# Twelve of the first batch's sixteen value pages loaded by SyncE, one in each of the units 82 to 93

## The chip, the core and the metric

The kernel runs on one core of a Trainium2 chip. The metric is the device time of one execution in microseconds; of the kernel before there are three runs, 997.36 to 998.01, with the median 997.86. The core has TensorE (PE, with PEld for the loads of its weights), VectorE (DVE), ScalarE (ACT), GpSimd (POOL) and SyncE (SP, which here only issues DMAs and waits), and 16 DMA engines that all queues share. Each engine runs its own list of instructions in order; they meet at semaphores.

## What is computed

A batch of 32 sequences of 32 tokens with 512 features gets a residual of a small per-subject matrix product (layer 0) and then a residual of attention over a paged cache (layer 1). Cut to what matters here:

```python
# x: (32, 32, 512); block_table: (32, 16) page numbers below 64
x = x + einsum('bct,bcd->bdt', x, weights[subjects])       # layer 0
q = rope(rmsnorm(x @ Wq.T)); k = rope(rmsnorm(x @ Wk.T)); v = x @ Wv.T
kc = k_cache[block_table].reshape(32, 512, 8, 128)         # 16 pages of 32 rows
vc = v_cache[block_table].reshape(32, 512, 8, 128)
k_all, v_all = concat(kc, k), concat(vc, v)
probs = softmax(where(valid, q @ k_all * SCALE, -1e30))    # 32 query heads on 8 key heads
x = x + (probs @ v_all) @ Wo.T
```

## The kernel before

**Stages.** The first stage runs 96 units (NU), twelve weight chunks by eight groups of four batches (NG = 8): units 0 to 79 (NN = 80) project queries and keys, units 80 to 95 the new values. A unit is twelve matmuls of 512 columns on TensorE. Beside them ScalarE and VectorE turn both caches into pairs of 16-bit numbers, high and low part, which SyncE stores into two tensors in device memory: k_pages_t (keys, one block per page) and v_pages, (2048 rows, 2048 elements), whose row is one cached token: 8 heads by high and low part by 128, 4096 bytes. A page is 32 rows, 128 KB.

The second stage is the attention: 256 steps i and a few to drain, four query heads of one batch to a step, eight steps to a batch. In step i TensorE does the transposes of the softmax rows of step i (L1585), the scores of step i + 3 (L1571 and L1575), and from step 3 on the products with the values of an earlier step (L1614); VectorE takes the maxima (L1267), ScalarE the exponentials (L1039), POOL multiplies the rows by the reciprocals of their sums (norm, L957). The scores of the steps 0 to 2 are computed already in the units 93 to 95.

**Where keys and values lie.** kt[b % 2] holds the keys of batch b, vs[b % 2] its values: `vs0` is 128 partitions by four chunks c of 4096 bytes; chunk c holds the pages 4c to 4c + 3, each on 32 partitions. TensorE's first scores of a batch wait for all its 16 key pages and its new keys (d_kt, 17 DMAs), its first product with values for the four gathers of the batch (d_vs).

**POOL.** After the last unit of the projections of keys, POOL waits for the stored caches (converted), for the row numbers v_row and for VectorE's count of 80 tiles (v_proj), then issues the four gathers of batch 0 (load_v, L944), each 128 rows by 4096 bytes by row number. Then it normalises rows 0 and 1, and in step 0 of its loop: row 2, a wait for the new values of batch 0 (d_vn, L989), a wait for the last projection (L993), the first gather of batch 1, and on to row 3.

**SyncE.** Its list is written out by hand, unit by unit. In unit u from 80 to 95 (NEXT_KEYS_AT = 80) it reads one page number into a register (TENSOR_LOAD, L716) and loads one key page of batch 1 (L721). In the units 84, 86 and 88 it loads 1 MB of output weights, four heads at a time (WO_LOADS, L734); ScalarE and VectorE convert two heads in each of the units 89 to 94 (L1082, L1315), so the third load is wanted in unit 93. In unit 83 it stores the row scales and in unit 87 loads them (L774), followed in unit 87 by the queries and new keys of batches 0 and 1 (L708, L710). In unit 93 it loads the new values of batch 0 (load_new_v, L730, three DMAs of 64 KB). Each unit ends with the store of the new values that VectorE staged for the unit before (v_new, L805, 256 KB), for which SyncE waits on v_proj. Behind the last unit: the last such store (L811), two more loads of output weights, a wait until all stores have landed, the new values of batch 1 (L730), and then for each batch b the queries of batch b + 2 (L708, after TensorE's count of scores), its 16 key pages (L721) and its new values.

## Time and profile before

| | |
|---|---|
| median of three runs | 997.86 us (997.36 to 998.01) |
| the profiled execution | 997.4 us, span of the core 995.6 us, mean granted TensorE clock 0.998 |
| TensorE matmuls, weight loads | 959.1 us busy (96%), 797.6 us (80%) |
| VectorE, ScalarE, POOL | 828.0 us (83%), 761.1 us (76%), 579.0 us (58%) |
| DMA | 294.92 MB, mean 296 GB/s over the span |
| SyncE's and ScalarE's DMA queue, POOL's queue | 76.4% and 18.2% of the 16 DMA engines' time |

All times below are microseconds from the start of the span. A line of a timeline has start, duration, engine, line of the code, operation, output <- input, and in brackets how long the engine was idle before and what ended that. SPq is SyncE's list of DMA issues; the duration of an issue is SyncE's own time, not that of the transfer. A DMA share of 1.00 means that all 16 DMA engines are busy. The projections end and the attention begins between about 338 and 356 us.

### The profile page before, as it was taken

What the parts mean: (1) busy time and instruction counts of PE and PEld (TensorE: products, weight loads), DVE (VectorE), ACT (ScalarE), POOL (GpSimd) and SP (SyncE); (2) the same over time, 40 slices, a digit from 0 to 9 for tenths busy, and PEclk for the clock granted to TensorE, in tenths of its full rate; (3) what the DMA queues carried; (4) which work ended last, traced back from release to release, by engine and by line L of the source; (5) the groups of instructions that cost most, each with busy time, mean ns of one, the idle gap of its engine ahead of it and who ended that gap; (6) DMA issues with size and microseconds to landing.
All of it is one profiled execution on the core that took longest, in us unless ns stands there. A gap on an engine that the chain in (4) does not pass through costs nothing.

```text
span 995.6 us, 25120 instructions
## 1 busy us (share of the span) xinstructions
PE 959.1 (96%) x8075; PEld 797.6 (80%) x8075; DVE 828.0 (83%) x1842; ACT 761.1 (76%) x2108; POOL 579.0 (58%) x861
## 2 busy tenths in 40 slices
PE   6899999999899999899999999999999999989998
PEld 4678888888677778788888888888888888878885
DVE  7789999999998689888878888888887887877880
ACT  5898999988884688888777778777877777777770
POOL 5565665655893057666755666565556555655550
PEclk9999999999999999999999999999999999999999
DMA  5899999989998989999999998999998999999950
GB/s 195 285 307 338 320 381 374 383 286 379 399 365 264 342 306 352 342 308 269 292 313 270 289 304 285 296 295 271 329 269 274 334 283 260 308 291 284 262 133 11
DMA packets 249907, 294.92 MB, mean 296 GB/s; under 512 B 79024, under 2 KB 206512, under 8 KB 247216
## 3 DMA queue, kind: packets, MB, share of 16 engines
q1 hardware_dynamic: 231088, 226.07, 76.4%
q0 software_dynamic: 18688, 67.25, 18.2%
q8 instruction: 65, 1.06, 0.4%
q14 instruction: 66, 0.54, 0.2%
HBM read 231.77 MB, written 46.27 MB: 279 GB/s over the span
## 4 chain that ended last, share of the span: by engine, by line
PE 75%; DVE 10%; POOL 6%; issue 5%; ACT 2%; DMA 2%; SPq 0%; DVEq 0%; ACTq 0%; POOLq 0%
PE ps_proj L1533 17%; PE ps_y L1533 16%; PE ps_o L1614 14%; PE ps_s L1571 8%; PE ps_t L1585 7%; PE ps_s L1575 7%; PE ps_rt L1709 2%; POOL vs L944 2%; DVE c_stage L1429 1%; POOL probs L963 1%; DVE rot L1405 1%; PE ps_o L1626 1%; DVE rot L1397 1%; DVE probs L1267 1%; DVE stage L1415 1%
## 5 line engine op out<-in xcount | busy, mean ns | idle before, releaser
L1039 ACT ACTIVATE probs<-probs,neg_max 128x544 f32<-128x544 f32 x256 | 191.6, 749 | 114.1 <-DVE neg_max L1267 97.3
L1267 DVE CUSTOM_DVE_ANT_0 probs<-ps_s,mask,row_scale 128x544 f32<-128x544 f32 x256 | 200.5, 783 | 52.3 <-PE ps_s L1575 41.2
L1614 PE MATMUL ps_o<-pt,vs 128*128 128x128 f16 x3072 | 213.3, 219 | 0.9 <-DMA vs<-v_pages,v_row 0.8
L1614 PEld LDWEIGHTS ps_o<-pt,vs 128*128 128x128 f16 x3072 | 192.4, 98 | 15.8 <-DMA vs<-v_pages,v_row 1.6
L963 POOL TENSOR_SCALAR probs<-probs,recip 128x512 f32<-128x512 f32 x144 | 99.8, 693 | 167.8 <-DVE recip L1275 164.2
L909 POOL TENSOR_TENSOR roped<-rot 128x256 f32<-128x256 f32 x160 | 144.1, 922 | 79.9 <-DVE rot L1397 75.9
L1533 PE MATMUL ps_proj<-wt_hi,x0t_hi 128*128 128x512 f32 x384 | 159.1, 415 | 6.2 <-DVE x0t_lo L1223 5.8
L1287 DVE SCALAR_TENSOR_TENSOR pt<-ps_t,pt 128x512 f16<-128x512 f32 x190 | 130.4, 686 | 36.7 <-ACT pt L1045 30.9
L1533 PE MATMUL ps_y<-wo,ot_hi 128*128 128x512 f16 x512 | 153.3, 381 | 0.0
L1533 PE MATMUL ps_proj<-wt_hi,x0t_lo 128*128 128x512 f32 x384 | 150.7, 394 | 0.0
L1533 PE MATMUL ps_proj<-wt_lo,x0t_hi 128*128 128x512 f32 x384 | 149.8, 391 | 0.0
L944 POOL DMA_INDIRECT vs<-v_pages,v_row x128 | 130.8, 1022 | 27.7 <-issue 9.4
L1571 PE MATMUL ps_s<-kt,qt 128*128 128x256 f16 (+1 forms) x768 | 136.0, 286 | 0.8 <-issue 0.7
L1045 ACT ACTIVATE pt<-ps_t 128x512 f16<-128x512 f32 x190 | 112.0, 590 | 24.9 <-PE ps_t L1585 18.3
L1575 PE MATMUL ps_s<-kt,qt 128*128 128x288 f16 (+1 forms) x768 | 125.8, 273 | 1.5 <-DVE neg_max L1267 1.4
L1585 PE MATMUL ps_t<-fixed,probs 128*128 128x128 f32 x760 | 115.5, 275 | 7.8 <-POOL probs L963 4.8
L1585 PEld LDWEIGHTS ps_t<-fixed,probs 128*128 128x128 f32 x760 | 91.9, 141 | 35.0 <-POOL probs L963 6.5
L1114 ACT ACTIVATE squares<-ps_proj 128x128 bf16<-128x128 f32 x320 | 85.3, 297 | 23.3 <-PE ps_proj L1533 23.2
L1533 PE MATMUL ps_y<-wo,ot_lo 128*128 128x512 f16 x256 | 97.0, 379 | 0.0
L1575 PEld LDWEIGHTS ps_s<-kt,qt 128*128 128x128 f16 x768 | 73.7, 98 | 20.2 <-DVE neg_max L1267 3.9
L1533 PEld LDWEIGHTS ps_proj<-wt_hi,x0t_hi 128*128 128x128 f32 x384 | 72.4, 189 | 20.9 <-DVE x0t_lo L1223 7.1
L957 POOL TENSOR_SCALAR probs<-probs,recip 128x544 f32<-128x544 f32 (+1 forms) x64 | 43.3, 676 | 76.1 <-DVE recip L1275 74.2
(162 smaller groups left out, 1811.8 us busy)
## 6 DMA issues: line engine op xcount, KB each, us to landing
kt<-k_pages_t SPq DMA_DIRECT2D x512, 128.0 KB
c_nat<-in_L_cond_k_cache SPq DMA_DIRECT2D x32, 512.0 KB, 6.0
q_t<-stage SPq DMA_DIRECT2D x64, 256.0 KB, 6.3
c_nat<-in_L_cond_v_cache SPq DMA_DIRECT2D x32, 512.0 KB, 7.2
qt<-q_t SPq DMA_DIRECT2D x32, 512.0 KB
w_nat<-in_L_cond_Wq SPq DMA_DIRECT2D x8, 1024.0 KB, 7.5
k_pages_t<-c_stage SPq DMA_DIRECT2D x16, 512.0 KB, 5.2
c_nat<-in_L_cond_Wo SPq DMA_DIRECT2D x16, 512.0 KB, 6.5
```

What stands on the lines that cost most here:

```text
L909: last = pool.tensor_tensor(dst, a, b, ALU.add)
L944: pool.indirect_dma_start(vs[b % 2][:, c].rearrange("p j s d -> p (j s d)"), None, v_pages, bass.IndirectOffsetOnAxis(ap=v_row[:, b * NCH ...
L963: pool.tensor_scalar(old_keys(i), old_keys(i), col(recip, i), 1.0, ALU.mult, ALU.mult).then_inc(p_old, 1)
L1039: act.activation(pr, pr, ACT.Exp, bias=col(neg_max, i), scale=-1.0, accum_out=col(row_sum, i)).then_inc(a_exp, 1)
L1045: act.activation(pt_part(i, 0), t_bank("t", i)[:], ACT.Copy, scale=P_SCALE).then_inc(a_thi, 1)
L1267: dve.tensor_tensor_reduce(out=probs_of(i), in0=ps_s[:, score_cols(i):score_cols(i) + KEYS], in1=mask[(i // HK) % 2][:, mask_at(i):mask_at ...
L1287: dve.scalar_tensor_tensor(pt_part(i, 1), t_bank("t", i)[:], P_SCALE, pt_part(i, 0), ALU.mult, ALU.subtract).then_inc(v_tlo, 1)
L1533: ins = pe.matmul(ps, a, b, start=first and n == 0, stop=last and n == len(pairs) - 1)
L1571: pe.matmul(own[0], q[:, a], k[:, b, own[1]:own[2]], start=n2 == 0, stop=n2 == 2)
L1575: ins = pe.matmul(shared[0], q[:, a], k[:, b, shared[1]:shared[2]], start=n2 == 0, stop=n2 == 2)
L1585: ins = pe.transpose(t_bank("t", i)[:, c * P:(c + 1) * P], probs_of(i)[:, SEQ * (i % 2) + c * P:SEQ * (i % 2) + (c + 1) * P], ident[:])
L1614: ins = pe.matmul(ps_o[n % 2][:, jl * P:(jl + 1) * P], v[:, part, :], pt[pt_slot(i)][:, NCH * half + c, :], start=jl == 1 and c == 0 and k ...
```

## The change

SyncE gets a second helper, load_value_pages, which reads one page number into a register and loads that page's 32 rows, 128 KB, into the 32 partitions and the chunk of vs[0] where they belong. It is called in each of the units 82 to 93, behind the key page of the unit, for the pages 4 to 15; in unit 82 SyncE first waits for VectorE's count of 80 tiles. POOL's gather for batch 0 keeps the chunk 0 alone. The first product with the values of batch 0 waits for the twelve pages (a semaphore of their own, d_vp) and for the one gather; the counts of the later even batches are three DMAs lower.

```diff
+    d_vp = sem("d_vp")
...
+    VALUES_AT = 82
...
+            def load_value_pages(first, count):
+
+                _, pages = nc.values_load_multi_w_load_instructions(
+                    page_ids[0:1, first:first + count], engines=[SP_ENGINE], min_val=0, max_val=PAGES - 1,
+                    skip_runtime_bounds_check_because="page_ids is clamped to the pages on the vector engine")
+                rows_of_page = v_pages.rearrange("(n t) f -> n t f", t=PSIZE)
+                for pg, page in enumerate(pages, first):
+                    c, a = divmod(pg, GB)
+                    sp.dma_start(vs[0][PSIZE * a:PSIZE * (a + 1), c].rearrange("p j s d -> p (j s d)"),
+                                 rows_of_page[bass.ds(page, 1)].rearrange("a t f -> (a t) f")).then_inc(d_vp, 16)
...
                 if NEXT_KEYS_AT <= u < NEXT_KEYS_AT + NPP:
                     load_pages(1, u - NEXT_KEYS_AT, 1)
+                if u == VALUES_AT:
+                    sp.wait_ge(v_proj, NN)
+                if VALUES_AT <= u < VALUES_AT + NPP - GB:
+                    load_value_pages(u - VALUES_AT + GB, 1)
...
             pool.wait_ge(v_proj, NN)
-            load_v(0, *range(NCH))
+            load_v(0, 0)
...
                 if j == 1:
-                    pe.wait_ge(d_vs[b % 2], 16 * NCH * (b // 2 + 1))
+                    if b == 0:
+                        pe.wait_ge(d_vp, 16 * (NPP - GB))
+                    pe.wait_ge(d_vs[b % 2], 16 * (NCH * (b // 2 + 1) - (0 if b % 2 else NCH - 1)))
```

## Rows read from the trace of the kernel before

**Rows 1.** Windows of core 0: length, busy us of each engine, PEclk, DMA share, GB/s.

```profile
312.00:330.00 18.00, 18.00 (x81) 14.52 (x80) 10.31 (x24) 6.14 (x10) 0.00 (x0) 1.00 1.04 353
330.00:344.00 14.00, 14.00 (x67) 11.17 (x65) 10.82 (x17) 11.54 (x19) 0.00 (x0) 1.00 1.05 385
344.00:352.00 8.00, 6.52 (x41) 4.46 (x38) 5.77 (x15) 5.64 (x12) 1.45 (x2) 1.00 0.34 105
352.00:376.00 24.00, 22.81 (x259) 20.13 (x258) 20.98 (x59) 20.26 (x48) 15.67 (x20) 1.00 1.02 347
```

**Rows 2.** Timeline of TensorE's weight loads (start, us, what, idle before, releaser).

```profile
375.36 0.22 PEld L1571 LDWEIGHTS ps_s<-kt,qt 128*128 128x128 f16 x3 [0.36 <-DMA kt<-k_pages_t]
```

**Rows 3.** Timeline of POOL, 305 to 354 us: gathers L944, normalisations L957.

```profile
305.80 1.11 POOL L944 DMA_INDIRECT vs<-v_pages,v_row  x1 [0.17 <-issue]
...
349.02 0.72 POOL L957 TENSOR_SCALAR probs<-probs,recip 128x544 f32<-128x544 f32 x1 [38.38 <-DVE recip L1275]
...
352.21 0.72 POOL L957 TENSOR_SCALAR probs<-probs,recip 128x544 f32<-128x544 f32 x1 [1.05 <-DVE recip L1275]
...
353.08 1.02 POOL L944 DMA_INDIRECT vs<-v_pages,v_row  x1 [0.15 <-issue]
```

**Rows 4.** Timeline of TensorE: the fourth transposes of the attention.

```profile
354.96 0.63 PE L1585 MATMUL ps_t<-fixed,probs 128*128 128x128 f32 x4 [0.63 <-issue]
```

**Rows 5.** Timeline of SyncE's DMA issues, 330 to 370 us.

```profile
330.35 0.34 SPq L734 DMA_DIRECT2D wo<-in_L_cond_Wo  x1
...
332.32 0.53 SPq L805 DMA_DIRECT2D v_new<-stage  x1
...
333.32 0.34 SPq L721 DMA_DIRECT2D kt<-k_pages_t  x1
...
333.72 0.53 SPq L805 DMA_DIRECT2D v_new<-stage  x1
...
340.47 1.27 SPq L730 DMA_DIRECT2D vn<-v_new  x3
...
351.09 0.51 SPq L811 DMA_DIRECT2D v_new<-stage  x1
...
354.39 1.28 SPq L730 DMA_DIRECT2D vn<-v_new  x3
...
358.34 0.34 SPq L708 DMA_DIRECT2D qt<-q_t  x1
...
360.52 9.10 SPq L721 DMA_DIRECT2D kt<-k_pages_t  x16
```

**Rows 6.** Time to landing: wo issued 330.35, wo issued 351.65 and 352.3, v_new issued 346.83.

```profile
DMA to landing us min/median/max: 8.4/8.4/8.4
...
DMA to landing us min/median/max: 6.0/6.0/6.0
...
DMA to landing us min/median/max: 2.4/2.4/2.4
```

**Rows 7.** Line L716, 305 to 345 us: SyncE's reads of page numbers, ns min/median/max.

```profile
L716 SPq TENSOR_LOAD <-page_ids x16: 265/274/907, 305.3 to 344.1; - x16
```

**Rows 8.** SyncE's waits, 305 to 330, then 330 to 360 us (total, times, longest).

```profile
SPq L751 <- DVE stage L1415: 5.1, 2, 3.4
...
SPq L811 <- DVE stage L1409: 3.7, 1, 3.7
...
SPq L708 <- PE ps_s L1575: 2.7, 1, 2.7
...
SPq L805 <- DVE stage L1409: 2.3, 2, 1.9
...
SPq L730 <- DMA v_new<-stage: 0.5, 1, 0.5
```

**Rows 9.** Timelines of VectorE and of ScalarE before the attention.

```profile
337.69 0.35 DVE L1505 TENSOR_SCALAR row_scale<-row_scale,s_unscale 128x256 f32<-128x256 f32 x1
...
341.61 1.32 ACT L1082 ACTIVATE wo<-wo,scale 128x512 f16<-128x512 f32 x2
```

## The prediction

> **What bounds the kernel now.** I read the windows table first. In the second half of the projections, 312 to 344 us, TensorE is busy every microsecond at the full clock (1.00, the 2.4 GHz level), and it is so again from 352 to 376 us apart from small gaps; between lies the turn from the projections to the attention, 344 to 352, where it loses about 1.5 us [rows 1]. The same table shows the second resource: the 16 DMA engines are full (1.04, 1.05) up to 344, nearly idle (0.34) from 344 to 352, and full again (1.02, 347 GB/s) from 352 to 376 [rows 1]. So until 344 no value load can be worth anything to TensorE, while after 352 TensorE and the DMA engines are both at their limit. Where do they meet? TensorE's weight load at 375.36, the first of batch 2's scores, waited 0.36 us and was released by the landing of batch 2's key pages [rows 2]. Those pages have no slack at all: that is the place by which I judge this change.
>
> **POOL's side.** Before, POOL issues four gathers from 305.80 on, about 1 us each, and then has nothing to do until the first softmax rows at 349.02; its work on batch 1's values begins at 353.08, right behind its third normalisation at 352.21 [rows 3]. Three gathers fewer cost POOL nothing and give nothing: the cover is its own idle time. The values of batch 0 are first read in step 3 of the attention, after TensorE's transposes at 354.96 [rows 4], and the last of the twelve pages is issued in unit 93, which is about 349 in the working below. With the 5.7 us that follow as the nearest latency (key page issues end at 360.52 + 9.10 = 369.62 and TensorE is released at 375.36 [rows 2, 5]) the last page would land at about 355, just in time; with the 2.4 us of a lightly loaded engine [rows 6], at 351.5. I take the light value, for the engines drain in this stretch. No gain, no cost.
>
> **SyncE's side.** A unit without a wait is one key page and one store of new values: from the store at 332.32 to the one at 333.72 are 1.40 us, of which the store takes 0.53, so a page costs SyncE 0.87 (0.34 for the issue at 333.32, the read of the page number, 0.274 in the middle of 16 such reads, and the steps between) [rows 5, 7]. A value page is the same pair of instructions, so I take 0.87. Bounds: 0.34 + 0.27 = 0.61 if the steps overlap, and 0.53 + 0.53 = 1.06 if its issue is as long as that of a store; single reads of page numbers took up to 0.907 [rows 5, 7]. The Trainium skill, "DMA: Bandwidth & Descriptors", section "Latency and other measured facts", gives a tensor_load a floor of about 600 ns; the row has 265 to 274 ns for most, so the row decides, but by the page each added page would cost 1.20 us, and SyncE would be 3.6 us later than I say.
>
> The twelve pages are in units 82 to 93. The one of unit 82 vanishes: before unit 83's store SyncE waits 3.4 us for VectorE [rows 8]. Eleven remain: 11 x 0.87 = 9.6 us. Queued behind them on SyncE are, in order:
> - the third load of output weights, issued at 330.35 behind six of the eleven (+5.2, so 335.6). It landed 8.4 us after its issue, with full engines [rows 5, 6]. ScalarE uses it at 341.61 [rows 9]. With 8.4 it would come 2.3 late; but SyncE now sends less per microsecond, so the backlog shrinks; with the 6.0 us of two such loads at 352 [rows 6] it is in time. I take 0, and keep 2.3 for the range.
> - the row scales and the queries of batch 0, +3.5: both are issued in unit 87, by 330. The scales are read by VectorE at 337.69 [rows 9], the queries by TensorE later still, in unit 93. Nothing.
> - the new values of batch 0 (340.47; a wait of 0.5 goes), +9.1: issued at 349.6 to 350.9. POOL waits for them ahead of the gather at 353.08 and of the normalisation that TensorE waits for at 354.96 (idle 0.63) [rows 3 to 5]. With the 2.4 us landing they are there at about 353.2: 0.2 to 1 us late. This one is on the path.
> - the last store of new values: it waited 3.7 us for VectorE, the one before about 1.9 [rows 8]. So 9.1 - 5.6 = 3.5 us late: 354.6 instead of 351.09.
> - two loads of output weights of 1 MB, right behind it, then batch 1's new values (354.39), then batch 2's queries and key pages, which waited 2.7 us for TensorE (358.34) [rows 5, 8]. The issue of batch 2's pages is thus only 3.5 - 2.7 = about 0.8 us late, plus what the longer landing of the last store adds: 1 to 2 us.
>
> **The sum goes by the DMA engines.** From 352 they are full, so batch 2's pages land when the bytes in front of them are through. What before was sent in the idle 344 to 352 is now sent later: of SyncE's list, one key page (128 KB) and two stores of 256 KB, some 0.65 MB, are issued after 352, at 347 GB/s 1.9 us [rows 1]. The 2 MB of output weights start 3.5 us later, and the stretch before them is fed with 384 KB per 1.40 us (0.27 of 0.35 MB per us) and one gather, so about 0.6 us of the engines is lost. Together 2.5 us; the pages had no slack [rows 2], so TensorE resumes at 375.4 + 2.5. The 0.2 to 1 us at step 3 lies ahead of this and is contained in it (TensorE comes later and waits less). Behind 376 TensorE is dense and everything that SyncE and POOL issue waits for TensorE's counts, so the shift stays: nothing gives it back. The profiled execution was 997.4 us (span 995.6 and 1.8 around it), the median of the runs 997.9; 997.9 + 2.5 = 1000.4.
>
> Bounds: with 0.61 per page, 6.7 - 0.5 - 5.6 = 0.6 us late at the last store, and the total is about +0.3. With 1.06, 11.7 - 6.1 = 5.6 late, about +4.6.
>
> **The rivals.**
> *Hidden.* SyncE's waits of 3.7, 2.3, 2.7 and 0.5 us are 9.2 together, nearly the 9.6 added [rows 8]. If the full engines before 344 are what stretches SyncE's issues (16 reads from 0.265 to 0.907), fewer bytes ahead shorten them by 1 to 2 us, the two stores go out before 352, and what remains is the 0.2 us at step 3: 998.1. For it: the added load is as large as the slack, not larger. Against it: the waits lie behind the loads, but the new values of batch 0 lie ahead of them and see the full 9.1.
> *Several things late.* Reads of 0.9 us, the third load of output weights 2.3 us late for ScalarE just when the softmax chain starts, new values 2 us late for POOL: 1.06 per page and more gives +4.6 to +6: about 1003. The Trainium skill, "SBUF — State Buffer", section "Door 1: The DMA port swizzle", says that a transfer's rate depends on how many of 16 ports its partitions reach, and 32 consecutive partitions reach 8. No row isolates a 32-partition transfer. As a mechanism of this kernel: twelve pages of 128 KB at 385 GB/s [rows 1] take 0.34 us each of the engines, at half the rate 0.68, so 4.1 us more in a stretch that was full; about half of it fits in the idle time the slower SyncE makes, the rest moves batch 2's pages: +4.5, 1002.4.
> *Faster.* The four gathers put 2 MB into the engines at 306 to 311, ahead of SyncE's list. If the later waits for DMAs come from backlog that never drains, sending 1.5 MB of it in pieces would let batch 2's pages land sooner. Place: the weight load at 375.36; price: its 0.36 us [rows 2], and at most some 2 us if other waits on values later share the cause: 996 to 997.5. It decides only if the engines have no idle time between; they have 5 us at 344 to 352 (0.34 busy) [rows 1], which wipes out any backlog. Little chance.
> *The change doesn't do what it says.* The pages might go out in one burst because SyncE waits at unit 82 for VectorE's count of 80 tiles; but POOL passed the same wait at 305.80 [rows 3], before SyncE gets there. No chance worth a number.
>
> **How the numbers follow.** Likeliest 0.60: +1 to +4, 1000.4. Hidden 0.25: within 1 us. Several late: 0.07, +4 and more; the port rule 0.03 beside it. Faster 0.05. The range of 8 in 10 runs from 997.9 (the low bound of the page's cost and the hidden case) to 1003.0 (the high bound). A measurement tells about 0.2%, 2.0 us, from no change. Of the likeliest case about three quarters lie above +2.0, and all of the two cases behind it: slower 0.55. Faster by over 2.0: 0.03. Same: 0.42.
>
> **What would show it.** SyncE's new page loads 0.87 us apart from their neighbours; the new values of batch 0 issued at 349 to 351; the last store near 354.6 with no wait before it; TensorE's weight load for batch 2's scores near 378 and released by the key pages, with a longer wait than 0.36; the windows 344 to 352 with a DMA share well over 0.34. The forecast is wrong if the last store is still released by VectorE at about 351, or if the pages land by 376 although SyncE is late: then bytes were not the limit.

## The result, and the profile after

| | before | after |
|---|---|---|
| median of the runs made beside each other | 998.01 us (13 runs, 996.50 to 999.44) | 1000.75 us (13 runs, 999.17 to 1004.55) |
| ratio with its 95% interval | | 1.0033 [1.0023, 1.0044] |
| profiled execution, its span, mean granted clock | 997.4, 995.6 us, 0.998 | 1004.55, 1002.8 us, 0.995 |
| the same kernel profiled again (e1_again, below) | | 1000.26, 998.5 us, 0.997 |

The changed kernel is slower: by 0.33% in the paired ratio, and by 2.7 us between the medians, where +2.5 us (0.25%) was forecast. Its first profiled execution was the slowest of its 13; the second, e1_again, lies near the median, and I read both.

The windows of the changed kernel that answer to [rows 1], with the same columns (length, busy us of PE, PEld, DVE, ACT, POOL, PEclk, DMA share, GB/s), first execution:

```profile
312.00:330.00 18.00, 18.00 (x81) 14.61 (x80) 10.10 (x23) 6.64 (x11) 0.00 (x0) 1.00 0.75 234
330.00:344.00 14.00, 13.74 (x65) 10.74 (x63) 9.11 (x14) 8.83 (x14) 0.00 (x0) 1.00 1.02 346
344.00:352.00 8.00, 3.24 (x10) 2.66 (x11) 4.02 (x7) 5.30 (x9) 0.00 (x0) 0.81 0.76 238
352.00:376.00 24.00, 22.74 (x237) 19.43 (x237) 20.46 (x57) 18.98 (x43) 14.37 (x19) 0.99 0.96 321
```

and of e1_again:

```profile
344.00:352.00 8.00, 5.64 (x33) 3.99 (x34) 5.75 (x14) 6.03 (x13) 1.45 (x2) 1.00 0.77 245
352.00:376.00 24.00, 22.78 (x258) 20.05 (x256) 20.99 (x58) 19.89 (x47) 15.09 (x20) 1.00 1.00 347
```

The values no longer fill the engines at 312 to 330 (0.75 instead of 1.04) and what SyncE sends late fills the gap at 344 to 352 (0.76, 0.77 instead of 0.34), as forecast. In the first execution TensorE works only 3.24 us of those 8, in the second 5.64, against 6.52 before.

Two waits carry the loss. The timelines of ScalarE and of TensorE's weight loads in the first execution (start, duration, what, and in brackets the idle time before with its releaser):

```profile
345.74 1.33 ACT L1099 ACTIVATE wo<-wo,scale 128x512 f16<-128x512 f32 x2 [4.57 <-DMA wo<-in_L_cond_Wo]
...
382.62 0.22 PEld L1588 LDWEIGHTS ps_s<-kt,qt 128*128 128x128 f16 x3 [3.13 <-DMA kt<-k_pages_t]
```

and in e1_again:

```profile
342.19 1.33 ACT L1099 ACTIVATE wo<-wo,scale 128x512 f16<-128x512 f32 x2 [1.77 <-DMA wo<-in_L_cond_Wo]
...
378.37 0.35 PEld L1588 LDWEIGHTS ps_s<-kt,qt 128*128 128x128 f16 x3 [2.78 <-DMA kt<-k_pages_t]
```

The first is ScalarE in unit 93, which before worked there at 341.61 without a wait [rows 9]: the third load of output weights comes late. The second answers to [rows 2]: batch 2's key pages, 0.36 us of waiting before, 3.13 and 2.78 now.

**How much is lost where.** Already at unit 80, ahead of the first changed instruction, the profiled executions lie up to 1.8 us to either side of the kernel before, so I count every time from ScalarE's work on unit 80. Its timeline in the kernel before, the work on unit 80 and an exponential of step 30:

```profile
301.81 0.69 ACT L1121 ACTIVATE stage<-ps_proj,scale 128x512 f16<-128x512 f32 x1 [2.19 <-PE ps_proj L1533]
...
409.43 0.75 ACT L1039 ACTIVATE probs<-probs,neg_max 128x544 f32<-128x544 f32 x1 [1.38 <-DVE neg_max L1267]
```

and in e1_again:

```profile
300.77 0.69 ACT L1138 ACTIVATE stage<-ps_proj,scale 128x512 f16<-128x512 f32 x1 [1.58 <-PE ps_proj L1550]
...
413.85 0.75 ACT L1056 ACTIVATE probs<-probs,neg_max 128x544 f32<-128x544 f32 x1 [1.59 <-DVE neg_max L1284]
```

That is 113.08 against 107.62 us: e1_again is 5.46 us late at step 30. The same count in every kernel gives a "shift" for the exponential of step 30, for that of step 224 and for the end of the span:

| kernel | third weight load issued | ScalarE's wait | last store issued | TensorE's wait, batch 2 | shift at 30 / 224 / end |
|---|---|---|---|---|---|
| before | 330.4 | none | 351.1 | 0.36 | 0 / 0 / 0 |
| after | 338.1 | 4.57 | 356.8 | 3.13 | 9.1 / 9.1 / 7.7 |
| e1_again | 337.2 | 1.77 | 355.0 | 2.78 | 5.5 / 5.4 / 3.9 |
| e2_third_ahead | 329.5 | none | 356.2 | 3.99 | 5.4 / 5.1 / 2.8 |
| e3_fifth_behind | 337.4 | 1.68 | 355.5 | 0.75 | 9.1 / 9.5 / 7.2 |
| e4_both | 328.9 | none | 354.9 | 1.47 | 5.6 / 5.6 / 3.3 |
| e5_gathers_spread | 332.8 | none | 351.2 | 0.28 | 0.1 / 0.6 / 0.6 |
| e6_reads_only (the kernel before once more) | 330.5 | none | 351.1 | none | 0.1 / -0.1 / 1.4 |
| e7_four_pages | 334.6 | 2.15 | 353.9 | 0.85 | 2.7 / 2.9 / 1.4 |
| e8_weights_behind_new_values | 337.6 | 4.83 | 357.8 | 1.79 | 7.7 / 7.7 / 5.5 |
| e9_weights_in_unit_95 | 330.3 | none | 351.1 | none | 1.0 / 1.0 / 1.0 |
| e10_issue_time_only | 338.5 | 2.03 | 358.2 | 3.67 | 9.3 / 9.1 / 10.0 |
| e11_three_small_gathers | 337.2 | 1.53 | 355.8 | 3.17 | 4.5 / 4.2 / 3.1 |
| e12_four_pages_third_ahead | 327.9 | none | 351.1 | 1.03 | 0.6 / 0.5 / -1.0 |

The loss at the front is 5.5 to 9.1 us, two to nearly four times the forecast. Between step 30 and step 224 next to nothing changes ("the shift stays"). Behind step 224 every kernel with fewer gathers than before, and e11, makes good some 2.3 us from one exponential to the next; in e1_again and in the first execution of the changed kernel 0.8 and 1.0 us of that are lost again a few steps on, where TensorE waits 0.65 and 0.82 us for values, so that 1.5 and 1.4 remain at the end. With e1_again's early unit 80 (-1.04) its 3.9 make the 2.9 us between the spans, 998.5 and 995.6.

**One execution is not the kernel.** e6_reads_only turned out to be the kernel before once more, and its trace ends 1.4 us later than that of before. TensorE waited 2.42 us in batch 27 in both; behind the wait its granted clock stayed at 1.00 in the one and fell in the other, which put 1.5 us on the exponentials. The window of e6 behind that wait:

```profile
891.00:895.00 4.00, 3.61 (x25) 3.18 (x26) 0.69 (x1) 1.08 (x2) 2.93 (x5) 0.57 0.93 282
```

A granted clock of 0.57 over 4 us is 1.7 us of the full clock lost. Such stretches stand at different places in different traces. The first execution of the changed kernel has two of them at the front (348 to 353 and 383 to 387 us), e1_again one (378 to 382), e3 three (346 to 350, and two together at 397 to 405), e4, e7 and e11 one each, e8 and e10 two each, e2, e5, e9 and e12 none. So a shift of one trace can hold up to 5 us of clock beside the waits, and differences of 1 to 2 us between shifts don't rank two kernels; the medians do.

All medians, each against runs of the kernel before on the same chip:

| kernel | median us (runs) | before | ratio |
|---|---|---|---|
| e1_again | 1001.47 (5) | 997.74 | 1.0037 [1.0024, 1.0050] |
| e2_third_ahead | 1001.86 (5) | 997.74 | 1.0044 [1.0031, 1.0057] |
| e3_fifth_behind | 1002.42 (6) | 997.74 | 1.0044 [1.0027, 1.0060] |
| e4_both | 1001.49 (7) | 997.74 | 1.0042 [1.0024, 1.0059] |
| e5_gathers_spread | 999.29 (12) | 997.52 | 1.0013 [0.9997, 1.0030] |
| e6_reads_only | 997.68 (12) | 997.52 | 1.0002 [0.9989, 1.0015] |
| e7_four_pages | 995.58 (12) | 997.52 | 0.9982 [0.9969, 0.9995] |
| e8_weights_behind_new_values | 1002.47 (6) | 997.52 | 1.0055 [1.0038, 1.0073] |
| e9_weights_in_unit_95 | 997.96 (12) | 998.17 | 1.0003 [0.9991, 1.0014] |
| e10_issue_time_only | 1006.62 (6) | 998.17 | 1.0094 [1.0074, 1.0114] |
| e11_three_small_gathers | 1000.38 (12) | 998.17 | 1.0026 [1.0013, 1.0039] |
| e12_four_pages_third_ahead | 996.06 (12) | 998.55 | 0.9978 [0.9965, 0.9991] |

### The profile page after: what moved, and what is told of

The parts are those of the page before. It is cut to its first block, busy times and chain, and to the rows that moved or that the text cites. A ratio compares the mean times of both kernels' runs of the same rounds, so it can differ in the third digit from the quotient of the medians.

```text
span 1002.8 us, 25165 instructions
## 1 busy us (share of the span) xinstructions
PE 961.1 (96%) x8075; PEld 800.1 (80%) x8075; DVE 828.2 (83%) x1842; ACT 761.9 (76%) x2108; POOL 576.3 (57%) x858
## 3 DMA queue, kind: packets, MB, share of 16 engines
q8 instruction: 65, 1.06, 0.4%
## 4 chain that ended last, share of the span: by engine, by line
PE 71%; DVE 10%; POOL 5%; issue 5%; DMA 4%; SPq 2%; ACT 2%; DVEq 0%; ACTq 0%; POOLq 0%
PE ps_proj L1550 17%; PE ps_y L1550 15%; PE ps_o L1633 13%; PE ps_s L1588 7%; PE ps_t L1602 7%; PE ps_s L1592 7%; PE ps_rt L1728 2%; DVE c_stage L1446 1%; POOL vs L961 1%; DVE probs L1284 1%; POOL probs L980 1%; DVE rot L1422 1%; DVE rot L1414 1%; PE ps_o L1645 1%; DVE stage L1432 1%
## 5 line engine op out<-in xcount | busy, mean ns | idle before, releaser
L961 POOL DMA_INDIRECT vs<-v_pages,v_row x125 | 128.0, 1024 | 24.6 <-issue 12.9
```

The source lines that it names most:

```text
L961: pool.indirect_dma_start(vs[b % 2][:, c].rearrange("p j s d -> p (j s d)"), None, v_pages, bass.IndirectOffsetOnAxis(ap=v_row[:, b * NCH ...
```

## The experiments

### e1_again: the changed kernel, unedited

> The changed kernel, not edited: a second profile of it. In the first one ScalarE waited 4.57 us for the third load of output weights (unit 93) and TensorE's weight load waited 3.13 us for batch 2's key pages, and the span was 7.2 us above that of before, while the median of the runs is only 2.7 us above. Theory A (output weights: the third load is queued behind SyncE's added loads and reaches ScalarE late): the wait of ScalarE is there again, 1.5 to 5 us, and the steps of the softmax chain from the first on are later by that much. Theory B (bytes: batch 2's key pages land late, the term of my sum): the wait for key pages is 2 to 3 us and ScalarE's wait is 0 to 1. Ratio to before 1.002 to 1.005 by both.

Measured: 1.0037. Both waits are there, so neither theory holds alone. SyncE's issues in its timeline:

```profile
344.16 0.52 SPq L822 DMA_DIRECT2D v_new<-stage  x1
345.16 0.35 SPq L723 DMA_DIRECT2D kt<-k_pages_t  x1
346.27 0.33 SPq L734 DMA_DIRECT2D vs<-v_pages  x1
346.66 0.53 SPq L822 DMA_DIRECT2D v_new<-stage  x1
...
349.15 1.34 SPq L743 DMA_DIRECT2D vn<-v_new  x3
...
353.94 0.61 SPq L828 DMA_DIRECT2D v_new<-stage  x1
354.59 1.10 SPq L747 DMA_DIRECT2D wo<-in_L_cond_Wo  x2
...
360.01 1.25 SPq L743 DMA_DIRECT2D vn<-v_new  x3
361.31 0.54 SPq L710 DMA_DIRECT2D qt<-q_t  x1
```

From store to store a unit now takes 2.50 us, against 1.40 [rows 5]: a value page costs SyncE **1.10 us**, not 0.87. The reads of page numbers say why (line, operation, count, ns min/median/max; L718 reads for the key page, L728 for the value page, which follows directly on the key page's issue):

```profile
L718 SPq TENSOR_LOAD <-page_ids x15: 263/276/1110, 305.3 to 352.5; - x15
...
L728 SPq TENSOR_LOAD <-page_ids x12: 264/538/1141, 309.2 to 348.0; - x12
```

The same read takes 276 ns in the middle behind a store and 538 ns right behind another issue. SyncE's waits, 330 to 362 us:

```profile
SPq L646 <- DMA v_new<-stage: 3.9, 1, 3.9
```

This is the wait until all stores have landed. In the kernel before no wait is listed there (the 0.5 us of [rows 8] belong to the load of new values in unit 93). Its two weight issues:

```profile
351.65 1.10 SPq L734 DMA_DIRECT2D wo<-in_L_cond_Wo  x2
```

From their end to the issue of the new values [rows 5] passed 354.39 - 352.75 = 1.6 us, and 360.01 - 355.69 = 4.3 us now. The last store is followed at once by 2 MB of output weights; SyncE stands 3.9 us in this wait with the queries and key pages of batch 2 behind it. Counted from unit 80, the queries go out at 362.35 (361.31 + 1.04) instead of 358.34: 4.0 late, and TensorE's weight load follows at 379.41 instead of 375.36: 4.05 late. The last page lands 5.5 us after its issue, 5.7 before: in this execution the transfer has not become slower, its issue has become later.

In the first execution it was otherwise. SyncE's waits there:

```profile
SPq L646 <- DMA v_new<-stage: 1.4, 1, 1.4
SPq L710 <- PE ps_s L1592: 1.0, 1, 1.0
```

TensorE was already 5.1 us late from ScalarE's wait, and SyncE, ahead of the queries, waited for it again. So its own lateness was covered there; the queries went out 5.1 us late, as late as TensorE. The 16 key pages then took 10.4 us from the first issue to the last (8.8 before, 9.1 in e1_again), and the last landed 7.1 us after its issue. The 1.6 and 1.5 us more than before cover what TensorE waited longer, 3.13 instead of 0.36. What made the issues and the landing slower in this execution isn't isolated by a run.

The remaining 1.4 us of e1_again's 5.5 are read from the windows of that wait, kernel before and e1_again:

```profile
378.00:382.00 4.00, 4.00 (x50) 3.62 (x48) 3.06 (x10) 3.31 (x9) 3.53 (x5) 1.00 1.01 359
```

```profile
378.00:382.00 4.00, 3.62 (x24) 3.11 (x25) 1.46 (x4) 0.90 (x3) 1.55 (x3) 0.57 1.00 391
```

Behind the 2.78 us in which TensorE stood still its granted clock is 0.57 over 4 us; 25 weight loads get done in place of 48. This doesn't follow every such wait: in e2, below, TensorE waited longer at the same place, 3.99 us, and kept the full clock:

```profile
381.00:385.00 4.00, 3.66 (x47) 3.43 (x48) 2.40 (x8) 1.44 (x4) 1.62 (x2) 1.00 0.99 344
```

### e2_third_ahead, e3_fifth_behind, e4_both: one late transfer at a time

e2 issues the third load of output weights in unit 87, ahead of the row scales and the queries; e3 sends the fifth behind batch 2's key pages; e4 does both.

```diff
-    WO_LOADS = {84: 0, 86: 1, 88: 2}
+    WO_LOADS = {84: 0, 86: 1}
+    THIRD_AT = 87
...
+                if u == THIRD_AT:
+                    sp.wait_ge(v_wlo, HPC * NCK)
+                    sp.wait_ge(t_proj, NU - NG)
+                    load_wo(2)
```

```diff
             load_wo(3)
-            load_wo(4)
             all_stored(sp)
...
                     load_pages(b + 2, 0, NPP)
+                if b == 0:
+                    load_wo(4)
```

> The changed kernel with the third load of output weights issued in unit 87 ahead of the row scales and the queries, instead of in unit 88 behind them and a value page: about 8 us earlier. Theory A: ScalarE's wait in unit 93 is gone, and with it most of the loss: within 0.8 us of before. Theory B: the wait for batch 2's key pages stays at 2 to 3 us and so does the time: 2 to 3 us above before. If both hold, half of the loss stays, 1 to 1.5 us.

> The changed kernel with the fifth load of output weights (1 MB, heads 16 to 19, wanted in step 25 of the attention) issued behind batch 2's key pages instead of ahead of them: 1 MB less in front of the pages, 3 us at 347 GB/s. Theory A: ScalarE's wait in unit 93 stays and the time stays, 2 to 3 us above before. Theory B: TensorE's wait for batch 2's key pages goes to 0 to 0.5 us, and the time comes to within 0.8 us of before.

> The changed kernel with both orders changed: third load ahead of the row scales, fifth behind batch 2's key pages. Theories A and B alike: nothing of the loss is left, within 0.6 us of before, or up to 0.4 us below it, for before itself waits 0.36 us for the key pages. A third theory, C (SyncE's late issue of batch 0's new values holds POOL in step 0 of the attention): 1 us above before stays, and POOL's third normalisation is followed by a gap of about 1 us.

Measured: 1.0044, 1.0044 and 1.0042; none is better than the changed kernel, and among themselves and from e1_again they can't be told apart. Timelines of TensorE's weight loads and of POOL in e2:

```profile
381.34 0.22 PEld L1591 LDWEIGHTS ps_s<-kt,qt 128*128 128x128 f16 x3 [3.99 <-DMA kt<-k_pages_t]
...
355.44 1.02 POOL L964 DMA_INDIRECT vs<-v_pages,v_row  x1 [1.67 <-DMA vn<-v_new]
```

ScalarE's wait is gone, but SyncE's list is as late as before, so TensorE, now earlier, waits 3.99 instead of 2.78 us at batch 2, and POOL 1.67 us for the new values. At step 5 e2 is level with the kernel before, from step 10 on it is 1.5 us late and at step 20 5.0. In e1_again ScalarE's wait was thus contained in the second one. TensorE's weight loads of batches 2 and 3 in e3:

```profile
377.06 0.22 PEld L1589 LDWEIGHTS ps_s<-kt,qt 128*128 128x128 f16 x3 [0.75 <-DMA kt<-k_pages_t]
...
398.92 0.34 PEld L1589 LDWEIGHTS ps_s<-kt,qt 128*128 128x128 f16 x3 [3.89 <-DMA kt<-k_pages_t]
```

1 MB less in front of batch 2's pages does let them land sooner (3.3 us after the last issue instead of 5.5) and takes 2 us of the wait away. But the megabyte and the late SyncE now meet batch 3's pages, and TensorE waits 3.89 us there. e4 has 1.47 and 3.81 in the two places. Up to step 15 it is 0.2 us late, at step 20 1.2 and from step 26 on 5.6, so nearly all of its loss stands at batch 3. (Theory C's gap of 1 us isn't there: POOL waits 0.36 us for batch 0's new values.) The bytes in front of the pages do count, then, 2 us for a megabyte, but they are paid for elsewhere. SyncE is behind on its list; to reorder what stands behind the added loads only chooses which batch pays.

### e5_gathers_spread: late bytes without SyncE's time

On the kernel before, POOL's four gathers go out at VectorE's counts of 80, 84, 88 and 92 tiles.

```diff
-            pool.wait_ge(v_proj, NN)
-            load_v(0, *range(NCH))
+            for c in range(NCH):
+                pool.wait_ge(v_proj, NN + 4 * c)
+                load_v(0, c)
```

> The kernel before, with POOL's four gathers of batch 0 not in a burst but one behind each fourth unit (VectorE's counts of 80, 84, 88 and 92 tiles): the bytes of the values come as late as in the changed kernel, without a microsecond of SyncE's time. Theory S (SyncE's time: what it issues late keeps the DMA engines idle before 352 and full behind it): within 0.8 us of before, and batch 2's key pages are waited for by under 0.7 us. Theory M (the moved bytes themselves, 1.5 MB later in front of the loads that matter): 2 to 3 us above before, with a wait for key pages of 2 us or more.

Measured: 1.0013 [0.9997, 1.0030], not told apart from the kernel before. A window and TensorE's weight load of batch 2:

```profile
344.00:352.00 8.00, 6.36 (x40) 4.47 (x38) 5.76 (x15) 5.68 (x12) 1.45 (x2) 1.00 0.72 241
```

```profile
375.31 0.22 PEld L1573 LDWEIGHTS ps_s<-kt,qt 128*128 128x128 f16 x3 [0.28 <-DMA kt<-k_pages_t]
```

The idle stretch is filled as in the changed kernel (0.72 against 0.77), the third weight load even goes out 2.4 us later than before, and batch 2's pages come as before. In the trace, values that are sent late cost the front 0.1 us, not 5.5. The medians are less sharp: they lie 1.8 us apart, where theory S said within 0.8, and the interval reaches up to 0.30%, which is within that of the change (0.23 to 0.44%). By the time alone part of the loss could be the values'; it is the trace, with a wait of 0.28 us for the key pages (under 0.7 by S, 2 or more by M) and no wait of ScalarE, that speaks for S.

### e6_reads_only: the reads of page numbers alone

It was meant to add two reads of page numbers in each of the units 82 to 93, with unused results.

> The kernel before, with two more reads of a page number by SyncE in each of the units 82 to 93, of which nothing is used: 0.8 to 1.1 us of SyncE's time a unit, no bytes moved. Theory S: it loses as the changed kernel does, 2 to 4 us above before, with the wait for batch 2's key pages of 2 to 3 us; ScalarE may wait 1 to 2 us for the third load of output weights. Theory M: within 0.8 us of before.

The expectation stays untested: the trace holds 62 reads of page numbers, all at the line of the key pages, as many as that of the kernel before; the added reads are not in it. It is the kernel before once more, and its ratio of 1.0002 [0.9989, 1.0015] shows how well the comparison holds. The question went to e10.

### e7_four_pages: a third of the dose

SyncE loads only the last four pages, in the units 82 to 85; POOL gathers three chunks.

```diff
-                if VALUES_AT <= u < VALUES_AT + NPP - GB:
-                    load_value_pages(u - VALUES_AT + GB, 1)
+                if VALUES_AT <= u < VALUES_AT + GB:
+                    load_value_pages(u - VALUES_AT + NPP - GB, 1)
...
-            load_v(0, 0)
+            load_v(0, 0, 1, 2)
```

> The changed kernel with only the last quarter's four pages by SyncE, in units 82 to 85, and three gathers by POOL. Three added pages behind the free one, 1.1 us each as the profile of the changed kernel shows (0.546 for the second read of a unit): SyncE is 3.3 us late, and its waits behind (1.9 and 3.7 us) take all of it. Theory S: within 0.7 us of before, the last store waits for VectorE by over 1 us. A rival, P (a transfer to 32 partitions is dear to the DMA engines): a third of the loss, 0.9 to 1.3 us.

Measured: 0.9982 [0.9969, 0.9995], **faster than the kernel before**. Timelines of ScalarE and TensorE's weight loads, and SyncE's wait for VectorE ahead of the last store:

```profile
343.36 1.33 ACT L1099 ACTIVATE wo<-wo,scale 128x512 f16<-128x512 f32 x2 [2.15 <-DMA wo<-in_L_cond_Wo]
...
377.85 0.22 PEld L1588 LDWEIGHTS ps_s<-kt,qt 128*128 128x128 f16 x3 [0.85 <-DMA kt<-k_pages_t]
```

```profile
SPq L828 <- DVE stage L1426: 3.6, 1, 3.6
```

SyncE catches up: it waits 3.6 us for VectorE ahead of the last store, as before (3.7, [rows 8]); that this store is 2.8 us later is VectorE's doing, which comes after ScalarE. Theory S had this right, and the third of the loss that theory P asks for (0.9 to 1.3 us) isn't there; a gain wasn't expected by either and is taken up at e11. The profiled execution, 998.25 us, was the second slowest of the twelve. What is left is the third weight load, 4.2 us later than before, and the 2.15 us that ScalarE waits for it. So the waits do hide added issues, as long as these end before the waits come; only the load that stands between is hit.

### e8_weights_behind_new_values

On the changed kernel, both loads of output weights go behind the wait for all stores and batch 1's new values.

```diff
-            load_wo(3)
-            load_wo(4)
             all_stored(sp)
             sp.wait_ge(d_x0, 16)
             load_new_v(1)
+            load_wo(3)
+            load_wo(4)
```

> The changed kernel with the fourth and fifth loads of output weights (2 MB) issued behind the wait for all stores and batch 1's new values instead of ahead. In the second profile of the changed kernel SyncE stood 3.9 us in that wait, because the stores' landing shared the engines with the 2 MB, and issued batch 2's queries 3 us later than before. Theory I (issue time: it is SyncE's lateness at batch 2's pages that counts): the pages are issued 2 to 3 us earlier, and the time comes to within 1 us of before. Theory B (bytes: the engines are full from 352 on whoever is first): the pages still land 3 us late, and the time stays 2 to 4 us above before.

Measured: 1.0055. SyncE's wait for the stores falls from 3.9 to 1.9 us, and it is back on the gate: it waits 1.9 us for TensorE's count before batch 2's queries. Timelines of ScalarE and of TensorE's weight loads:

```profile
344.86 1.33 ACT L1099 ACTIVATE wo<-wo,scale 128x512 f16<-128x512 f32 x2 [4.83 <-DMA wo<-in_L_cond_Wo]
...
381.49 0.22 PEld L1588 LDWEIGHTS ps_s<-kt,qt 128*128 128x128 f16 x3 [1.79 <-DMA kt<-k_pages_t]
```

The key pages' wait is a microsecond shorter than in e1_again, and between steps 15 and 20 the shift grows by 1.2 us, where it grew by 3.8 and 4.2 in the two executions of the changed kernel. But ScalarE waited 4.83 us in this execution, as in the first one of the changed kernel (4.57), where e1_again had 1.77; the third load took 8.9 us to land (8.2 and 6.0 in those two). One execution can't say whether the edit or the spread between executions made that, since everything that it changes stands behind unit 93 on SyncE; the time shows no gain.

### e9_weights_in_unit_95: the idle engines filled

On the kernel before, the last two weight loads are issued in unit 95, ahead of its key page and the last stores.

```diff
+                if u == NU - 1:
+                    load_wo(3)
+                    load_wo(4)
...
-            load_wo(3)
-            load_wo(4)
             all_stored(sp)
```

> The kernel before, with the fourth and fifth loads of output weights (2 MB) issued in unit 95, ahead of the store for which SyncE waits for VectorE, instead of behind the last store: about 6 us earlier, into the stretch 344 to 352 in which the DMA engines are idle. If bytes in front of batch 2's key pages set their landing (theory B), TensorE's wait for them (0.4 to 1 us before) is gone and the waits for values of the batches behind are shorter: 0.5 to 2.5 us below before. If it is issue time (theory I), nothing changes, within 0.5 us. Against both: batch 0's new values and ScalarE's weights could be late behind 2 MB, 1 us above before.

Measured: 1.0003 [0.9991, 1.0014]. A window, and TensorE's weight load of batch 3:

```profile
344.00:352.00 8.00, 6.52 (x35) 4.39 (x34) 5.95 (x14) 6.04 (x12) 0.73 (x1) 1.00 0.96 329
```

```profile
395.74 0.22 PEld L1572 LDWEIGHTS ps_s<-kt,qt 128*128 128x128 f16 x3 [1.55 <-DMA kt<-k_pages_t]
```

The share at 344 to 352 rises from 0.34 to 0.96, batch 2's last page lands 2.6 us after its issue instead of 5.7, and TensorE no longer waits for those pages. Nothing is gained: the pages' issue is gated by TensorE's count of scores (SyncE waits 2.9 us for it), the steps up to 22 of the attention follow each other within 0.05 us as before, and the next batch's pages are then waited for, 1.55 us, which makes this execution 1.0 us late at step 30. 2 MB out of the way bring 3 us of earlier landing and no time. That is not a hard test of my sum: the kernel before waits only 0.36 us for these pages, so there was no more than that to gain at batch 2.

### e10_issue_time_only: SyncE's time without the bytes

On the kernel before, SyncE gets the same pair of instructions in the units 82 to 93, a read of a page number and a load from that page, but of 512 bytes, into a spare tensor in device memory.

```diff
+                if 82 <= u < 94:
+                    _, pages = nc.values_load_multi_w_load_instructions(
+                        page_ids[0:1, u - 78:u - 77], engines=[SP_ENGINE], min_val=0, max_val=PAGES - 1,
+                        skip_runtime_bounds_check_because="page_ids is clamped to the pages on the vector engine")
+                    rows_of_page = v_pages.rearrange("(n t) f -> n t f", t=PSIZE)
+                    sp.dma_start(spare[u - 82], rows_of_page[bass.ds(pages[0], 1), 0:16, 0:16].rearrange("a t f -> (a t) f")
+                                 ).then_inc(d_sp, 16)
```

> The kernel before, with one more read of a page number and one DMA of 512 bytes (device memory to a spare place there) by SyncE in each of the units 82 to 93, behind the key page: the instructions of a value page without its bytes; POOL gathers all of batch 0 as before. SyncE's added time is that of the changed kernel, 1.1 us a unit. Theory S (SyncE's time): the softmax chain and batch 2's key pages are late as in the changed kernel, TensorE waits 2 to 3 us for the key pages, and from step 17 on the steps are 3 to 5 us later than before; with the stall of POOL's 122nd gather still there, 3 to 5 us above before. Theory M (moved bytes, or transfers to 32 partitions): under 1 us above before, the wait for key pages under 1.2 us.

Measured: 1.0094 [1.0074, 1.0114], **nearly three times the loss of the change, with next to no bytes added**. SyncE's issues, then ScalarE and TensorE's weight loads, then a window:

```profile
333.19 0.58 SPq L797 DMA_DIRECT2D spare<-v_pages  x1
```

```profile
342.22 1.33 ACT L1092 ACTIVATE wo<-wo,scale 128x512 f16<-128x512 f32 x2 [2.03 <-DMA wo<-in_L_cond_Wo]
...
382.16 0.35 PEld L1581 LDWEIGHTS ps_s<-kt,qt 128*128 128x128 f16 x3 [3.67 <-DMA kt<-k_pages_t]
```

```profile
344.00:352.00 8.00, 5.59 (x32) 3.95 (x33) 5.76 (x14) 6.03 (x13) 1.45 (x2) 1.00 0.52 151
```

The same two waits stand in the same two places, although the DMA share at 344 to 352 is 0.52, less than with the values (0.77), and 151 GB/s. The dose is larger than the change's: the little issue takes 0.56 to 0.58 us where a value page's takes 0.33, the unit from store to store 2.80 us where it takes 2.50, and the last store goes out at 358.2, 3.2 us later than in e1_again. POOL also waits 1.5 us for the new values of batch 0 here. So this run doesn't price the change; it shows that the loss needs none of the values' bytes. With e5 this settles which of the two it is: the values late without SyncE's time cost the front nothing in the trace and at most 0.30% in the medians, SyncE's time without the values costs at least as much as the change. What the pair doesn't separate is SyncE's lateness from its other transfers, the key pages and stores, being sent late with it: e10 has both.

### e11_three_small_gathers: what is given back

Between step 224 and the end the changed kernel makes good 1.4 to 1.5 us, which is 2.3 less the 0.8 to 1.0 lost again behind it. POOL and TensorE there, kernel before:

```profile
888.45 1.03 POOL L944 DMA_INDIRECT vs<-v_pages,v_row  x1 [2.84 <-PE ps_o L1614]
```

```profile
890.30 0.66 PE L1585 MATMUL ps_t<-fixed,probs 128*128 128x128 f32 x4 [2.42 <-POOL probs L963]
```

and the same gather in e7_four_pages:

```profile
888.50 1.03 POOL L961 DMA_INDIRECT vs<-v_pages,v_row  x1 [0.51 <-POOL ptn L995]
```

This is POOL's 122nd gather of the kernel. Where POOL has 136 gathers in all (before, e5, e6, e9, e10) it starts some 2.3 us late and TensorE waits 2.42 to 2.44 us for the normalisation behind it. In the changed kernel and its relatives, with 133 or 135, the wait is 0.4 to 1.2 us, and all eight of their traces show the same 2.3 us made good at this place. To see whether the count does it, e11 added three small gathers of 16 KB to the changed kernel, 136 again:

```diff
             load_v(0, 0)
+            for g in range(3):
+                pool.indirect_dma_start(spare[:], None, v_pages.rearrange("n (c f) -> (n c) f", f=64),
+                                        bass.IndirectOffsetOnAxis(ap=v_row[:, g:g + 1], axis=0)
+                                        ).then_inc(d_more, 16)
+                pool.wait_ge(d_more, 16 * (g + 1))
```

> The changed kernel with three more gathers by POOL, of 16 KB each into a spare tile, in POOL's idle time behind the one gather of batch 0: POOL issues 136 gathers in all, as in the kernel before, instead of 133. In every profile with 136 gathers so far (three kernels) POOL's 122nd gather, in batch 27, starts 2.3 us later than its place asks for and TensorE waits 2.42 us; in none of seven profiles with 133 or 135. Theory Q (the place in POOL's list of gathers sets it): the stall is back at the 122nd gather, and the time is 1 to 2.3 us above the changed kernel's. Rival (something else of the change, such as when the loads fall, keeps it away): no stall, and the time of the changed kernel within 0.8 us.

Measured: 1.0026 [1.0013, 1.0039]. POOL and TensorE in e11:

```profile
911.40 1.03 POOL L963 DMA_INDIRECT vs<-v_pages,v_row  x1 [2.86 <-issue]
```

```profile
913.25 0.66 PE L1609 MATMUL ps_t<-fixed,probs 128*128 128x128 f32 x4 [0.49 <-POOL probs L987]
```

A gap of the same size is back, 2.86 us, but at the 126th gather, where TensorE waits only 0.49 us and the exponentials come 1.2 us later. At the 122nd there is none, and the 2.3 us are made good as with 133 gathers: theory Q, the place in the list, doesn't hold. The time can't be told apart from the changed kernel's (1.0026 and 1.0033). So the gathers' number or size plays a part in whether and where POOL pauses; the cause of the pause stays open, and whether every execution has it isn't known: the kernel before has two traces, its own and e6, both with the late gather and the wait of 2.42 us, the changed one has two without it, and the others have one each.

### e12_four_pages_third_ahead: what the experiments point to

e7's four pages, and e2's third weight load in unit 87, ahead of the row scales and queries.

> Four value pages by SyncE in units 82 to 85 (one gather less for POOL), and the third load of output weights in unit 87 ahead of the row scales and queries. The kernel with four pages alone was 0.18% below before, although in its profile ScalarE waited 2.2 us for the third load; that profile has no stall of POOL's gather in batch 27, which costs the kernel before 2.4 us of TensorE. If the wait of ScalarE is what four pages still cost, this kernel is 1.5 to 4 us below before and below the kernel with four pages; if the third load ahead only makes the queries and new values late in its place, as with twelve pages, it is as the kernel with four pages, 0.5 to 2.5 us below before. Were the stall back, it would be equal to before.

Measured: 0.9978 [0.9965, 0.9991], faster than the kernel before and 0.55% faster than the changed one by the two ratios (0.9978 / 1.0033). Its profile has no wait of ScalarE for the weights, the last store at 351.1 as before, and a shift of 0.6 us at step 30 and -1.0 at the end: 2.3 us are made good where the pause of batch 27 is gone, and 0.8 lost again behind it. Against e7 (0.9982) it can't be told apart. So the traces show no gain from the values' new way in the projections; what they do show is the 122nd gather. That it makes the medians' 0.2% is argued from its size, 2.3 us, and not shown by a run of its own.

## Why it came out so

**Right.** The pages out of POOL's list gave and cost nothing at the front. The idle stretch filled up (0.76). The last store was forecast at 354.6 and went out at 355.0 in e1_again (counted from unit 80), with no wait for VectorE ahead of it. The place by which the change was to be judged, the weight load of batch 2, was released by the key pages, with a longer wait than 0.36. Nothing gave the shift back up to step 224. The total of +0.25% lies in the measured interval, 0.23 to 0.44%; that is in part luck, as the errors below show. The weight load at 378.37, forecast near 378, is luck too: e1_again was 1.04 us early at unit 80, and counted from there the load is 4.05 us late, not 2.5.

**Wrong: the price of a page.** 0.87 was forecast with 1.06 as the upper bound; it is 1.10. The mis-sized part is the read: I took its time behind a store (0.274) for one behind an issue (0.538 in the middle). The Trainium skill, "DMA: Bandwidth & Descriptors", "Latency and other measured facts", whose floor of some 600 ns gave 1.20 us a page, was nearer to the sum than my rows; its floor is still not what the trace shows, where the shortest read takes 0.263 us.

**Wrong: the third load of output weights, cost 0.** It was put 5.2 us late; it is 6.9 to 7.7, and it landed 6.0 and 8.2 us after its issue. I took the 6.0 of the loads at 352 and called 2.3 a bound; ScalarE waited 1.77 in one execution and 4.57 in the other. That difference is most of what lies between the two profiled executions (shifts 5.5 and 9.1).

**Wrong: the sum by the engines' bytes.** "0.65 MB carried into the full stretch, 1.9 us, and 0.6 us of idle engines" isn't how the time was lost in e1_again: the pages landed 5.5 us after their issue, 5.7 before. What failed is the step before: "the issue of batch 2's pages is only 0.8 us late, plus 1 to 2 us". It is 4.0 us late: the last store 3.9, the wait for its landing 2.7 more than before, less the 2.7 us that SyncE used to wait for TensorE; TensorE itself is 1.6 us late by then (ScalarE's wait) and waits for the rest. Bytes have a part in it all the same, since the store lands among 2 MB of weights in a stretch with full engines, and moving 1 MB (e3, e4) brought the landing from 5.5 down to 3.3 and 3.8 us. In the first execution SyncE's issue was no later than TensorE, and it was slower issues and landings, 1.6 and 1.5 us, that made the wait. So the root, SyncE's time, is shown; which share of the wait at batch 2 is late issue and which is slow landing differs from one execution to the other.

**The new values of batch 0, put "on the path" with 0.2 to 1 us.** They were issued at 350.2 in e1_again (forecast 349.6 to 350.9), but no wait of POOL for them stands in either trace of the changed kernel, where ScalarE's wait had made everything behind it late. Where that wait was gone, in e2, POOL waited 1.67 us for them and the steps were 1.5 us late from step 10 on.

**The port rule among the rivals.** The rule (the Trainium skill, "SBUF — State Buffer", "Door 1: The DMA port swizzle") isn't needed either: e10 has no transfer to 32 partitions and loses more. No run isolates such a transfer, so the rule itself is neither shown nor refuted here.

**Not foreseen: something given back.** The front lost 5.5 us (9.1 in the first execution) instead of 2.5, and the total came out right because 1.4 to 1.5 us are given back from batch 27 on, where the 122nd gather no longer starts late (2.3 us, less 0.8 to 1.0 of a new wait for values). "Nothing gives it back" was argued from how the attention is gated and holds up to step 224; a stall that the kernel before had by itself, 540 us further on, wasn't looked for.

## What to carry to other kernels

An engine that only issues DMAs is a resource with a price per instruction: count its free time (its waits) and note where in its list the waits stand. Added issues are hidden by the waits behind them, but everything between the addition and the first wait moves by the full amount. Bytes in front of a wanted transfer count as well (2 us for a megabyte here), but taking them away helps only where something waits for that transfer. When such a queue is late, reordering what follows only moves the wait to the next consumer; take a smaller dose, one that ends before the first wanted transfer. And read a total that matches a forecast by its stages: here two errors, one of +3 us and one of -1.5 us, lay beneath it. Profile the same kernel twice before ranking variants by their traces: two executions of one program ended 1.4 us apart.

## What was not expected of the hardware

- A register read from SBUF by SyncE took 0.276 us in the middle behind a store's issue (0.263 to 1.110), and 0.538 us in the middle right behind another load's issue (0.264 to 1.141).
- Twelve reads and issues of 512 bytes each cost 0.94% of the time; they took SyncE as long as, or longer than, those of 128 KB (0.58 us against 0.33 us an issue).
- After TensorE had stood still for 2.78 us, its granted clock over the next 4 us was 0.57 on average, between its two levels (full 2.4 GHz, the other 1.2): some 1.4 us beside the wait itself. After 3.99 us in e2 it stayed at 1.00; and after 2.42 us in batch 27 it stayed there in one execution of the kernel before and was 0.57 in the other (e6).
- POOL's pause of some 2.3 us before one late gather came and went, or moved, with gathers that had been issued 580 us earlier; why is open.
